# Attention row sums: half of the ones product moved to GpSimd and VectorE, and the row of maxima issued ahead of the store

## The reference

```
xn = layernorm(x)
q, k, v = xn Wq' + bq,  ctx Wk' + bk,  ctx Wv' + bv        # 16 heads of 32
p = softmax(q k' / sqrt(32));   a = (p v) Wo' + bo
x1 = x + tanh(g_xattn) * a
xf = layernorm(x1), fake-quantized to 8 bits with one scale for the whole tensor
h  = silu(xf Wg') * (xf Wu'), fake-quantized the same way   # 1408 wide
out = x1 + tanh(g_ffn) * (h Wd')
```

## Time and profile before

| what | value |
|---|---|
| median of 3 runs | 1844.71 us (1842.28 to 1851.07) |
| the profiled execution | 1839.49 us, its span 1837.7 us |
| TensorE matmuls busy | 1634.8 us (89%) |
| VectorE busy | 1288.7 us (70%) |
| ScalarE busy | 846.9 us (46%) |
| GpSimd busy | 517.8 us (28%) |
| row transfers, stacks<-mT | 16, median 4.1 us from issue to landing |

### The profile page before, as it was taken

The page is one execution under the profiler, slowest core; times in us unless marked ns, Lnnn a source line. Parts: engine busy times, 40 slices in busy tenths (PEclk is TensorE's granted clock), DMA queues, the critical chain, the costliest instruction groups (busy, mean ns, idle before and its releaser), DMA issues.

```text
span 1837.7 us, 33988 instructions
## 1 busy us (share of the span) xinstructions
PE 1634.8 (89%) x11880; PEld 769.5 (42%) x11880; DVE 1288.7 (70%) x2055; ACT 846.9 (46%) x1132; POOL 517.8 (28%) x782
## 2 busy tenths in 40 slices
PE   3859999899999999999999999946699999989887
PEld 2324444444444444444454444423344444434333
DVE  6727677776776777777767767657787778778555
ACT  3223534435335244253353352426777777755242
POOL 6114324234134243242341432202000000007644
PEclk7979999999999999999999999987799999989999
DMA  6649567577486586675865954543145543016897
GB/s 189 166 137 180 127 162 175 145 174 158 138 186 137 152 186 152 169 161 144 190 142 134 196 137 116 127 166 125 37 180 219 202 171 132 23 47 259 338 419 297
DMA packets 274971, 307.57 MB, mean 167 GB/s; under 512 B 152112, under 2 KB 201264, under 8 KB 272304
## 3 DMA queue, kind: packets, MB, share of 16 engines
q1 hardware_dynamic: 274864, 306.00, 59.5%
HBM read 176.17 MB, written 95.94 MB: 148 GB/s over the span
## 4 chain that ended last, share of the span: by engine, by line
PE 50%; issue 25%; DMA 9%; DVE 8%; POOL 3%; SPq 2%; ACT 2%; DVEq 0%; POOLq 0%; ACTq 0%
PE bank L1322 12%; PE bank L1223 10%; PE bank L1225 10%; PE bank L1224 10%; PE spair L1304 5%; DMA x<-out_dram 4%; DMA stacks<-mT 4%; POOL yh L625 3%; PE spair L1279 2%; DVE mx L917 2%; ACT pr L668 1%; DVE ndev L960 1%; DMA hb<-in_L_ffn_w_gate_dram 1%; PE bank L1214 1%; DVE xres L937 1%
## 5 line engine op out<-in xcount | busy, mean ns | idle before, releaser
L668 ACT ACTIVATE pr<-spair 128x1024 f32<-128x1024 f32 x256 | 259.3, 1020 | 182.4 <-PE spair L1304 182.4
L917 DVE TENSOR_REDUCE mx<-spair 128x4 f32<-128x1024 f32 x256 | 301.5, 1219 | 57.4 <-PE spair L1279 56.9
L895 DVE SCALAR_TENSOR_TENSOR parts<-bank,bqk,parts 128x512 f16<-128x512 f32 x128 | 96.1, 751 | 241.5 <-ACT parts L657 235.9
L1304 PE MATMUL spair<-stacks 128*128 128x256 f16 x1024 | 161.3, 287 | 53.5 <-DMA stacks<-mT 44.2
L1420 PE MATMUL spair<-xqT,wgT 128*128 128x512 bf16 x704 | 182.5, 382 | 1.2 <-ACT xqT L781 1.2
L1420 PE MATMUL spair<-xqT,wuT 128*128 128x512 bf16 x704 | 182.1, 381 | 0.0
L657 ACT ACTIVATE parts<-bank,bqk 128x512 f16<-128x512 f32 x128 | 88.0, 687 | 172.4 <-PE bank L1225 172.3
L1322 PE MATMUL bank<-pr,v 128*32 128x256 f32 x2048 | 143.1, 399 | 27.0 <-DVE o L911 25.2
L764 ACT ACTIVATE sil<-spair,gsc 128x512 f32<-128x512 f32 x176 | 118.2, 680 | 75.6 <-PE spair L1420 75.5
L1304 PEld LDWEIGHTS spair<-stacks 128*128 128x128 f16 x1024 | 91.6, 101 | 143.7 <-DMA stacks<-mT 51.8
L535 POOL TENSOR_TENSOR cl<-cbuf,ch 128x512 f16<-128x512 f32 x64 | 77.0, 1207 | 259.1 <-ACT ch L645 258.9
(11 more groups left out here) (172 smaller groups left out, 3273.7 us busy)
## 6 DMA issues: line engine op xcount, KB each, us to landing
stacks<-qk_spill SPq DMA_DIRECT2D x384, 128.0 KB, 4.2
qk_spill<-parts SPq DMA_DIRECT2D x64, 512.0 KB, 3.0
x<-out_dram SPq DMA_DIRECT2D x32, 1024.0 KB, 11.0
h_spill<-hb SPq DMA_DIRECT2D x10, 2816.0 KB, 9.2
hb<-h_spill SPq DMA_DIRECT2D x10, 2816.0 KB, 15.3
xbuf<-in_x_dram SPq DMA_DIRECT2D x16, 1024.0 KB, 6.9
cbuf<-in_ctx_dram SPq DMA_DIRECT2D x16, 1024.0 KB, 6.6
xres<-in_x_dram SPq DMA_DIRECT2D x16, 1024.0 KB, 5.6
```

The source lines that it names most:

```text
L668: act.activation(pr[:, u % 4, :, :, :].rearrange("p a b q -> p (a b q)"), spair[u % 2][:, :, :].rearrange("p a q -> p (a q)"), ACT.Exp, sc ...
L895: dve.scalar_tensor_tensor(out=parts[:, c, 2 * w + 1, :], in0=pj[(g + 1) % 3][:, :], scalar=bqk[:, w, c:c + 1], in1=parts[:, c, 2 * w, :], ...
L917: dve.tensor_reduce(mx[:, h:h + 2, b, :], spair[u % 2][:, :, :].rearrange("p a (q k) -> p a q k", q=KH), AX_X, ALU.max).then_inc(max_done, 1)
L1304: last = pe.matmul(spair[u % 2][:, a, kh * S:kh * S + S], kst[:, h, b * S + kh * P:b * S + kh * P + P], qst[:, h, b * S:b * S + S], start= ...
```

## The change

The store of x1 of a group is issued behind the next group's row of maxima. In each step, GpSimd adds the two key halves of the exponentials of the first two heads and VectorE those of the last two, into a new buffer ph of 128 x 4 x 256 fp32, of which there is one. The ones product then has 4 matmuls instead of 8, reads ph, and waits for both additions. An addition waits for its exponentials and for the step before to have read ph. In the pv step the values product stands first as before. GpSimd's low parts of ctx and x and of the attention result stand one step further back, and the additions stand in front of them; VectorE's addition for a step stands right behind the norm of the step before. For the text, addition g is the one for step g.

```diff
+        ph = alloc(p1, "ph", [P, 2, 2, S], F32)
...
             def body(i, j, par, more, first=False):          # SyncE
                 mrow(j)
+                if not first:
+                    store_x1(j - 1)
                 spill(i, 0)
...
-                store_x1(j)
...
             mrow(NG - 1)
+            store_x1(NG - 2)
...
+            def add_even(j, g):
+
+                wait(pool, exp_done, j * NU + 2 * g + 1)
+                wait(pool, pv_mm, j * NGR + g + 2)
+                pool.tensor_tensor(ph[:, 0, :, :], pr[:, (2 * g) % 4, :, 0, :], pr[:, (2 * g) % 4, :, 1, :],
+                                   ALU.add).then_inc(even_added, 1)
...
             def body(j, nxt):                                # GpSimd
+                add_even(j, 0)
                 for g in range(NGR):
+                    if g + 1 < NGR:
+                        add_even(j, g + 1)
                     if nxt is not None:
-                        if g < NT:
-                            low_c(nxt, g)
-                        else:
-                            low_x(nxt, g - NT)
-                    if g > 0:
-                        o_low(j, g - 1)
+                        if 1 <= g <= NT:
+                            low_c(nxt, g - 1)
+                        elif g > NT:
+                            low_x(nxt, g - NT - 1)
+                    if g > 1:
+                        o_low(j, g - 2)
                     if g == 2 and nxt is not None:
                         x_rstds(nxt)
                     if g >= NT:
                         residual(j, g - NT)
+                o_low(j, NGR - 2)
+                if nxt is not None:
+                    low_x(nxt, NT - 1)
                 o_low(j, NGR - 1)
                 x1_rstds(j)
...
+            def add_odd(j, g):
+
+                wait(dve, exp_done, j * NU + 2 * g + 2)
+                wait(dve, pv_mm, j * NGR + g + 2)
+                dve.tensor_tensor(ph[:, 1, :, :], pr[:, (2 * g + 1) % 4, :, 0, :], pr[:, (2 * g + 1) % 4, :, 1, :],
+                                  ALU.add).then_inc(odd_added, 1)
...
                     x1_shifts(before)                        # VectorE
+                add_odd(j, 0)
                 for g in range(NGR - 1):
                     norm(j, g)
+                    add_odd(j, g + 1)
...
-                for ones in (False, True):                   # TensorE, pv
-                    for kh in range(KH):
-                        for a in range(HPC):
-                            h = HPC * c + a
-                            at = S if ones else 0
-                            last = pe.matmul(obank[DK * a:DK * a + DK, at:at + S],
-                                             onesP[:, :] if ones else v[:, 2 * b + kh, DK * h:DK * h + DK],
-                                             pr[:, (2 * g + a // 2) % 4, a % 2, kh, :],
-                                             start=(kh == 0), stop=(kh == KH - 1))
+                for kh in range(KH):
+                    for a in range(HPC):
+                        h = HPC * c + a
+                        pe.matmul(obank[DK * a:DK * a + DK, 0:S], v[:, 2 * b + kh, DK * h:DK * h + DK],
+                                  pr[:, (2 * g + a // 2) % 4, a % 2, kh, :], start=(kh == 0), stop=(kh == KH - 1))
+                wait(pe, even_added, j * NGR + g + 1)
+                wait(pe, odd_added, j * NGR + g + 1)
+                for a in range(HPC):
+                    last = pe.matmul(obank[DK * a:DK * a + DK, S:2 * S], onesP[:, :],
+                                     ph[:, a // 2, a % 2, :], start=True, stop=True)
                 last.then_inc(pv_mm, 1)
```

More of the change, by code:

```diff
@@ L191, in gated_block_kernel @@
         exp_done = sem("exp_done")
+        even_added = sem("even_added")
+        odd_added = sem("odd_added")
         pv_mm = sem("pv_mm")
```

## The result

The changed kernel takes 1867.4 us (median of 4 runs, 1859.8 to 1871.8) against 1845.1 for the kernel before (4 runs): ratio 1.011, 95% interval 1.007 to 1.016. It is slower by 22 us; I had forecast 1832, faster. The profiled execution has a span of 1868.2, against 1837.7.

The account below looks back on a forecast made before the run. It took TensorE as the bound late in a group, with VectorE's chain and transfers bounding its start. Middle groups -9 and the first -3.3 gave -12.4 us: 1827 profiled, 1832 forecast for the median, range 1792 to 1856.

Parts of the forecast that it names:

- S to e0: From SyncE's issue of the x1 store to the end of PV step 0: -0.25 us per middle group.
- e0 to e4: End of PV step 0 to end of step 4, with additions in VectorE's chain: +1.04 us per middle group.
- e4 to e7: End of PV step 4 to end of step 7, TensorE-bound at 4.97 per step: -1.40 us per middle group.
- e7 to the next S: End of PV step 7 to the next group's start, seven blocks of projections and maxima: left alone.
- the entry: Group start to end of PV step 0: VectorE's addition waits for root and GpSimd; gain 0.25 us.
- rival D: Moved pause in step 0 puts half-speed TensorE into full work: +1.05 us per group, 1847 us; chance 0.13.
- The cut: Eight of 16 ones-product records dropped per PV step on TensorE: 0.465 us per step, 59.5 us at most.
- Steps 1 to 4: VectorE's additions and spreads (ndev) blocked by GpSimd instructions: step 4 ends 23.2 us after step 0, against 22.16.
- Rival C: VectorE's chain in steps 1 to 3 catches more of GpSimd: deciding from 0.9 more per group, 1865 us; chance 0.17.
- Rival B: Additions and spreads do not meet, or in an order costing nothing: -3.5 us per middle group, 1791 us; chance 0.25.
- The first group: First attention group, without spreads or root: 7 x 0.465 = -3.3 us, its entry 0.
- The last group: Last attention group: entry and two steps -1.8 us, then VectorE the bound and three additions +2: 0.

Follow-up runs that it names:

- e9: Changed kernel with thrown-away products filling TensorE's pauses before ones product 0 and values products 2 and 3: 1840.2 us, ratio 0.9978.
- e3: e1 with a four-matmul ones product over the first key half, no additions, second half left out: 1749.0 us, 0.9476. (In timings: end of PV step 3.).
- e1: Kernel before with only the store of x1 moved behind the row of maxima: 1796.6 us, ratio 0.9735.
- e7: Changed kernel, x1's root behind GpSimd's first addition, VectorE's first addition ahead of q/k part 1, its root wait behind norm 0 and addition 1: 1810.0 us, 0.9790.
- e2: In timings: end of PV step 2. As a run: changed kernel with the x1 store back in its old place, 1857.6 us, ratio 1.0066.
- e8: Changed kernel with the spreads (ndev) moved from VectorE to ScalarE: 1839.8 us, ratio 0.9963.
- e5: Changed kernel with GpSimd's addition only; the other two heads summed from both key halves on TensorE: 1899.0 us, ratio 1.0280.
- e6: Changed kernel with VectorE's addition only; the other two heads summed from both key halves on TensorE: 1829.9 us, ratio 0.9905.
- e4: Changed kernel with VectorE's addition replaced by a one-input reduction over the first key half, the second left out: 1864.9 us, ratio 1.0094.
- e13: Changed kernel, x1's root behind GpSimd's first addition, x1_shifts behind VectorE's first norm, spreads on ScalarE, maximum of x1 uncut: 1775.1 us, ratio 0.9624.

## Why the prediction was wrong

| part, per middle group | predicted | measured |
|---|---|---|
| S to e0, clock left out | -0.25 | +0.41 |
| S to e0, falls of before that are gone | 0 | -0.70 |
| e0 to e4, clock left out | +1.04 | +1.22 |
| e0 to e4, new falls | 0 | +2.00 |
| e4 to e7 | -1.40 | -1.30 |
| e7 to the next S | 0 | +0.17 |
| sum | -0.6 | +1.8 |

The clock's terms are worked out group by group from the same records. Before, five of the 14 entries hold no half speed and take 8.86 to 9.05, mean 8.96; the other nine take 10.05 on the mean: 1.09 x 9/14 = 0.70. Afterwards nine entries hold up to 1.9 us of half speed, nearly all while TensorE stands, and take 9.35 to 9.47; the five without take 9.28 on the mean, so 0.1 of the 0.41 is clock too. Step 1 takes 6.1 to 7.8 in 10 of the 14 groups and 5.00 in the others; step 4 takes 6.4 to 6.6 in 5 and 5.00 in the others: 1.45 + 0.55 = 2.00. e9 confirms that: it has no half speed, and a group takes 2.05 less, 27 us in all. These numbers are of one execution each. The parts outside the attention groups, which the change leaves alone, differ by over 6 us between the two, so some us of the terms may be of the execution.

The step that failed is the forecast's zero for the clock: the sum had only the entry, steps 0 to 4 and steps 4 to 7, all at full speed. I had it as rival D, with a chance of 0.13 and +1.05 per group for a fall moved from the entry to step 1. It came, a little larger: +1.30, since a second place was added (the pauses of 1.4 and 2.0 ahead of values products 2 and 3, and the fall in step 4). That is 18 of the 35 us between 1832 and 1867. I rated it low although I had both of its halves: the falls of before behind a pause of 2.5, and a new pause of the same kind right in front of full work. Its price for a fall was low too: "up to 1.3", where the nine entries with one were 0.5 to 2.2 longer than the others.

Point by point:

- The cut, 0.465 per step: nearly right where TensorE is the bound (5.00 against 5.43, which is 0.43, and e3).
- The entry: right in its chain, and 0.66 too good, 9 us of the miss. The root ended at S + 6.56 (I had 6.64), GpSimd added until S + 8.03 (7.95), VectorE until S + 8.72 (8.6); from there to e0 it took 0.78, not 0.51. That is 0.39 in the group read; the rest of the 0.66 is that its entry before, 9.05 in the table's count, was above the mean of the undisturbed ones (8.96), and what clock is left afterwards. What I did not ask is what the row's 2 us would be worth without the additions: 46 us (e1). My "gain 0.25, although up to 2 us go" was the largest loss in the list; e7 gets it back with three calls moved.
- Steps 1 to 4: the collisions came nearly as worked out, +0.18 over the 14 groups. In the 13 that are alike it is +0.38 (5.00, 6.51, 7.07 and 5.00 against 5.43, 5.43, 5.87 and 5.43); the last, whose steps 2 and 3 lose nothing, pulls the mean down. In the group shown the spreads of step 1 end at e0 + 8.3 (8.0), e2 is e0 + 11.5 (11.1), values product 3 starts at e0 + 17.1 (16.6), e3 is e0 + 18.7 (18.0). The two spreads of step 1 took 2.57 (2.25); in step 2 the long wait fell on a 4-column scaling (1.08) instead of on the first spread. In step 1 GpSimd's addition 2 waits for the exponentials and starts 0.4 later than I had it.
- The Trainium skill's rule of exclusion (SBUF — State Buffer, section SBUF: two separate sides) has VectorE and GpSimd exclude each other for a whole instruction; the trace agrees, both ways: 2.57 against 0.99 for the two spreads, and 1.53 against 1.30 for GpSimd's addition where the spreads came first.
- Rival C, the chain catching more, needed 0.9 per group and got 0.2 to 0.4. That its 1865 lies next to the measured 1867 is chance. Rival B, no collisions, falls with the same rows.
- The first group kept 0.4 of its 3.3 up to e7: step 1 took 6.26 at half speed, and in step 3 two 4-column scalings were held up by GpSimd's addition and subtraction. The last group won 1.1 where I had 0.
- Late steps and SyncE's queue: as said. GpSimd's addition 4 had its slack behind the root only because VectorE's chain was later still; with the spreads away it is what ends last (e8).

Summed: 18 for the clock, 9 the entry, 2.5 the chain, 1.4 the late steps, 2.4 behind e7, 2.9 the first group, less 1.1: 35. (The forecast's three terms add to -0.61 per group, where it took -0.65; that is 0.6 us.)

What is not settled: why the fall comes in some groups and not in others with the same pause. The group shown first stood for 2.88 and had step 1 at full speed; the one at 712.92 stood for 2.93 and had not. Nor do the runs show where the 0.17 behind e7 comes from. They narrow it down: it is missing with either addition alone (e5, e6) and with a one-input addition on VectorE (e4), so it needs both, and VectorE's with two SBUF inputs. The additions' remaining price in e13 was read from its rows, not tried.

## What to carry to other kernels

Ask of each gain what else the same chain could have taken: here a transfer that lands 2 us earlier was worth 46 us, and vanished because a new wait took its place. Where a change opens a pause in TensorE in front of work that is bound by TensorE, give the clock a price of its own in the forecast; it is cheap to try: fill the pause with products nobody reads. Work moved off the bound engine costs what it blocks besides what it takes: look for the instructions of the neighbour, short ones too, that will stand beside it, and for the long helper (a root of twelve instructions) that stands in front of it.

## What the hardware showed that I had not expected

- Tiny instructions can be held as long as large ones. Two 4-column scalings of VectorE, 0.17 alone, took 1.29 and 1.08 beside GpSimd's addition and subtraction (e5), a 4-column one with two SBUF inputs 1.24. When two GpSimd instructions followed each other at once, VectorE got one instruction in between them in the rows shown (e5, 522.04 and 523.30).
- A 16 KB transfer issued 0.5 behind a 1 MB store in the same queue lands in 4.1, without the store ahead in 2.1 (medians of 16, kernel before and e1).
- Leaving the second key half of two of four heads on TensorE (e5, e6) gave nothing: steps of 5.43 and 5.42, against 5.43 with all eight ones matmuls and 5.00 with four. The products of the four heads write to four quarters of the bank's partitions, and two of them take the time of four.
- Thrown-away products on TensorE made the changed kernel faster by 27 us (e9).
